# Attention of 16 heads over 512 keys with its scores computed once, stage semaphores cleared one block later, a router's counting in bf16, and another order in the last block

## The reference, cut to what matters

```python
q, k, v = h @ wq, h @ wk, h @ wv             # (2, 512, 16, 64) each
scores = einsum('bqhd,bkhd->bhqk', q, k) / sqrt(64)
w = softmax(scores, axis=-1)
z = z + einsum('bhqk,bkhd->bqhd', w, v).reshape(2, 512, 1024) @ wo + bo
```

## Time and profile before

| what | us |
|---|---|
| three executions, median | 4797.91 |
| the profiled execution, its own time | 4793.56 |
| span of the profiled execution, first to last instruction | 4791.7 |
| granted TensorE clock over the span, share of full speed | 0.902 |
| from the start of the attention's first stage to the end of its main one | 341.9 |
| one of its 16 pairs of heads, in the middle | 19.12 |
| the router's counting on PE | 15.8 |

### The profile page before, as it was taken

How to read it: one execution, slowest core, us unless ns; L and a number is a source line. 1 busy time by engine, 2 the same in 40 slices (tenths; PEclk the granted TensorE clock), 3 DMA queues, 4 the chain that set the end, 5 groups by cost and what they waited for, 6 DMA issues and landing times. The chain is left out here.

```text
span 4791.7 us, 86667 instructions
## 1 busy us (share of the span) xinstructions
PE 4050.0 (85%) x24901; PEld 2629.4 (55%) x25261; DVE 3436.7 (72%) x17352; ACT 2225.4 (46%) x7299; POOL 396.3 (8%) x322
## 2 busy tenths in 40 slices
PE   8999999999999998938888888888874349789797
PEld 6888888888888887622333333333332235423356
DVE  6888888888888888547677777777764449744443
ACT  4555555555555555415555555555553212133232
POOL 0000000000000000020111111111100000023310
PEclk9999999999999999958888888888886559899998
DMA  0000000000000000122222222212210001100001
GB/s 29 2 2 2 2 2 2 2 2 2 2 2 2 2 2 2 34 60 52 48 52 48 52 48 52 45 44 47 44 33 5 4 1 38 35 10 11 8 14 40
DMA packets 80809, 105.31 MB, mean 22 GB/s; under 512 B 25599, under 2 KB 73914, under 8 KB 78395
## 3 DMA queue, kind: packets, MB, share of 16 engines
q1 hardware_dynamic: 80379, 100.28, 8.6%
HBM read 69.17 MB, written 30.26 MB: 21 GB/s over the span
## 5 line engine op out<-in xcount | busy, mean ns | idle before, releaser
L287 DVE CUSTOM_DVE_ANT_0 I-219junk<-I-215encw,I-218expo,I-227rec 128x77 f32<-128x77 f32 x3072 | 941.2, 356 | 6.3
L1315 DVE TENSOR_REDUCE I-41383nmax<-ps 128x1 f32<-128x512 f32 x768 | 500.9, 684 | 215.9 <-PE ps L984 209.4
L1203 ACT ACTIVATE I-41386prob<-ps 128x512 f32<-128x512 f32 x768 | 428.4, 596 | 227.8 <-PE ps L1021 145.7
L265 ACT ACTIVATE I-217tanh_s<-ps 128x77 f32<-128x77 f32 x1024 | 241.3, 236 | 595.1 <-PE ps L245 595.1
L245 PE MATMUL ps<-I-212hist,I-49small 128*128 128x77 f32 x2048 | 456.5, 305 | 40.7 <-DVE I-212hist L323 40.6
L245 PEld LDWEIGHTS ps<-I-212hist,I-49small 128*128 128x128 f32 x2048 | 305.0, 188 | 296.4 <-DVE I-212hist L323 296.3
L251 PE MATMUL ps<-I-217tanh_s,I-49small 128*128 128x77 f32 x2048 | 454.8, 304 | 0.0
L252 PE MATMUL ps<-I-212hist,I-49small 128*128 128x128 f32 x2048 | 440.0, 297 | 0.0
L247 PE MATMUL ps<-I-212hist,I-216uh_h 128*128 128x128 f32 x2048 | 439.8, 296 | 0.0
L984 PE MATMUL ps<-I-41377kS,I-41376qS 96*128 96x512 bf16 x768 | 331.2, 457 | 127.8 <-DVE I-41383nmax L1315 58.7
L273 ACT ACTIVATE I-223hh<-I-229gate_t,I-228pre,I-222rh 128x1 f32<-128x1 f32 x1024 | 395.3, 386 | 84.6
(11 more groups left out here) (534 smaller groups left out, 7254.4 us busy)
## 6 DMA issues: line engine op xcount, KB each, us to landing
I-41376qS<-parts SPq DMA_DIRECT2D x24, 768.0 KB, 7.5
parts<-I-41395room SPq DMA_DIRECT2D x36, 384.0 KB, 2.5
parts<-I-41395room SPq DMA_DIRECT2D x36, 256.0 KB, 2.2
I-41377kS<-parts SPq DMA_DIRECT2D x12, 768.0 KB, 7.9
parts<-I-41395room SPq DMA_DIRECT2D x36, 128.0 KB, 1.8
I-49small<-in_layers SPq DMA_DIRECT2D x6, 768.0 KB, 9.0
I-66646w<-in_blocks SPq DMA_DIRECT2D x8, 514.0 KB, 7.1
I-41376qS<-I-41385mrow SPq DMA_DIRECT2D x192, 2.0 KB
```

The source lines that it names most:

```text
L287: return e.tensor_tensor_reduce(junk[:, 2 * g + b, :], encw[:, g, b, :], expo[:, b, :], inv[:, b:b + 1], rec[:, b, g:g + 1], ALU.mult, ALU ...
L1203: e.activation(prob[:, tau % 2, j, :], k.ps[:, b, :], ACT.Exp, scale=scale).then_inc(free[b], 1)
L1315: e.tensor_reduce(nmax[:, U % HG, i, j:j + 1], k.ps[:, use[0], :], AX.X, ALU.max, negate=True).then_inc(free[use[0]], 1)
```

## The change

`stage` no longer clears its semaphores before a second barrier. The clears stand behind the block and are followed by no barrier, so POOL executes them at the head of the next stage while the other engines go on; the semaphores themselves are given back only when the next block has ended. At the end of the program one barrier stays.

`attention3` is replaced by `self_attention`, whose unit is one tile of 128 queries of a pair of heads: 64 units, unrolled. Per unit: two score matmuls (queries on partitions); DVE takes the maximum of both heads and scales it; ACT takes the exponential with the maximum as bias and sums over the keys at the same time (`accum_out`); DVE inverts the two sums per query; POOL multiplies the probabilities by them; PE transposes 8 tiles; ACT copies those of head 0 and DVE those of head 1 to SBUF; two matmuls per key tile multiply by V with all 512 queries. The first stage of before is gone, `wos` is loaded behind the third weights.

```diff
@@ stage
-        for sem in sems:
-            nc.gpsimd.sem_clear(sem)
-        nc.all_engine_barrier()
+    with nc.Block() as block:
+        yield block, sems
+    release()
+    for sem in sems:
+        nc.gpsimd.sem_clear(sem)
+    HELD.append(ctx)
@@ router
-        mask = sbuf(ctx, nc, "mask", [P, NT, E])
+        mask = sbuf(ctx, nc, "mask", [P, NT, E], BF16)
-                    for i in range(NT):
-                        for j in range(i + 1):
-                            mm = e.matmul(psp[:, i // TPB, i % TPB, :], k.tri if j == i else k.ones, mask[:, j, :],
-                                          start=(i % TPB == 0 and j == 0), stop=(j == i), skip_group_check=True)
+                    e.matmul(earlier, tri_b[:], mask[:], start=True, stop=False, skip_group_check=True)
+                    for j in range(NT - 1):
+                        mm = e.matmul(earlier[:, j + 1:, :], ones_b[:], mask[:, j:j + 1, :].to_broadcast([P, NT - 1 - j, E]),
+                                      start=False, stop=(j == NT - 2), skip_group_check=True)
...
-                    link(e.max(best[:, i, :], pr[:, i, :]))
+                    e.max(best[:, i, :], pr[:, i, :]).then_inc(s.best, 1)
...
-                    for b in range(B):
-                        link(e.tensor_scalar(keepb[:, b], psp[:, b], float(capacity), None, ALU.is_lt))
+                    link(e.tensor_scalar(keep[:], earlier, float(capacity), None, ALU.is_lt))
@@ self_attention (new), tensor
+                def flip(u):
+                    e.wait_ge(s.divided, u + 1)
+                    for a in range(2):
+                        if u:
+                            e.wait_ge((s.flat0, s.flat1)[a], u)
+                        for c in range(TPB):
+                            mm = e.transpose(k.ps[:, 6 + a, c * P:(c + 1) * P], prob[:, u % 3, a, c * P:(c + 1) * P], k.ident)
+                        mm.then_inc(s.flipped, 1)
...
+                for t in range(NU + PV):
+                    G, i = divmod(t, TPB)
+                    if t < NU:
+                        score(t)
+                    if i < 3 and G + 1 < NG:
+                        project(G + 1, i)
+                    if 0 <= t - LAG < NU:
+                        flip(t - LAG)
+                    if t >= PV:
+                        weigh(*divmod(t - PV, TPB))
@@ scalar
+                def raise_(u):
+                    e.wait_ge(s.topped, 2 * u + 2)
+                    if u >= 3:
+                        e.wait_ge(s.flipped, 2 * (u - 2))
+                    for a in range(2):
+                        e.activation(prob[:, u % 3, a, :], score_ps(u)[:, a, :], ACT.Exp, scale=scale,
+                                     bias=nmax[:, u % 2, a:a + 1], accum_out=total[:, u % 3, a:a + 1]).then_inc(s.raised, 1)
...
+                for t in range(NU + LAG):
+                    G, i = divmod(t, TPB)
+                    if i < 3 and G + 1 < NG:
+                        keep(G + 1, i)
+                    if t < NU:
+                        raise_(t)
+                    if t >= LAG:
+                        flatten(t - LAG)
@@ vector
+                def top(u):
+                    e.wait_ge(s.scored, u + 1)
+                    if u >= 2:
+                        e.wait_ge(s.raised, 2 * (u - 1))
+                    e.tensor_reduce(nmax[:, u % 2, :], score_ps(u), AX.X, ALU.max, negate=True).then_inc(s.topped, 1)
+                    e.wait_ge(s.topped, 2 * u + 1)
+                    e.tensor_scalar(nmax[:, u % 2, :], nmax[:, u % 2, :], scale, None, ALU.mult).then_inc(s.topped, 1)
...
+                for t in range(NU + PV + 1):
+                    G, i = divmod(t - PV, TPB)
+                    if t < NU:
+                        top(t)
+                    if G >= 1 and i == 0:
+                        keep_out(G - 1)
+                    if 0 <= t - LAG < NU:
+                        flatten(t - LAG)
+                    if t < NU:
+                        invert(t)
@@ gpsimd
+                for u in range(NU):
+                    e.wait_ge(s.inverted, u + 1)
+                    e.tensor_tensor(prob[:, u % 3], prob[:, u % 3], inv[:, u % 3, :].unsqueeze(2).to_broadcast([P, 2, T]),
+                                    ALU.mult).then_inc(s.divided, 1)
```

More of the change, by code:

```diff
@@ L2678, in _ @@
                 e.activation(eq[:], low[:], ACT.Exp).then_inc(s.exps, 1)
-                e.wait_ge(s.rows, 1)
-                for b in range(B):
-                    e.activation(place_row[:, b * T:(b + 1) * T], k.ps[:, 2 + b, :], ACT.Copy).then_inc(s.place_row, 1)
                 def pick(n):
@@ L2692, in _ @@
                         pick(n + 1)
+                    if n == 0:
+                        e.wait_ge(s.rows, 1)
+                        for b in range(B):
+                            e.activation(place_row[:, b * T:(b + 1) * T], k.ps[:, 6 + b, :], ACT.Copy).then_inc(s.place_row, 1)
                     if n < E:
@@ L2718, in link @@
                     e.wait_ge(s.step, done[0])
-                e.wait_ge(s.logits, 1)
-                link(e.tensor_tensor(lg[:], scores, each(bias), ALU.add))
-                link(e.tensor_reduce(most[:], lg[:], AX.X, ALU.max))
-                e.tensor_tensor(low[:], lg[:], over(most), ALU.subtract).then_inc(s.lowered, 1)
                 e.wait_ge(s.consts, 1)
@@ L2729, in _ @@
                 done[0] += 4
[L2730 to L2733 removed]
+                e.wait_ge(s.step, done[0])
                 for j in range(NSLOT):
```

413 lines of the change are left out of this document (142 added, 271 removed).

## The result

| | before | after |
|---|---|---|
| median of the runs, us | 4797.91 | 4665.59 |
| all runs, us | 4793.68 to 4799.32 | 4665.13 to 4668.61 |
| span of the profiled execution, us | 4791.69 | 4666.76 |

Forecast: 4669, range 4650 to 4702. To see whether the sum is right for its reasons, I cut both traces at the stage ends, and compared stage by stage the time from first to last work, and the idle time of all engines between two stages.

The account below looks back on a forecast made before the run. No engine was taken to bound the whole kernel; PE bounded the old attention. Gains of 75 (attention), 40 (stage ends), 15 (routers), less 1 (last block), made 129 us: 4664.6 on the profiled scale, 4669 on the median's, range 4650 to 4702.

Parts of the forecast that it names:

- The loop that was forecast: Attention: DVE's small scaling multiplication waits for POOL's multiplication; then exponentials, reciprocal and hand-overs, 1.8 us, make a 3.8 us period.
- P: Attention: time of POOL's multiplication of the probabilities per unit, taken as 2.0 us.
- flatten (and every fourth unit keep_out) fit beside the exponentials: Attention, DVE: these steps were taken to fit beside ACT's two exponentials, 1.5 us, adding nothing to the loop.
- PE's own price: Attention: PE's scores, transpositions, products with V and projections, 14.8 us a pair, 3.71 us a unit.
- PE bounds the attention: Rival: two elements don't take the ports, or POOL's multiplication is under 1.9 us; 4660 us in all; chance 0.18.
- 3.8 a unit: Attention: period of one of 64 units, set by the loop through POOL; 4.15 us upper end, PE's 3.71 lower.
- The start and the end: Attention: time of the stage outside its 64 unit periods, taken as 23 us (18 to 31).
- One meeting of the engines, 0.25: Stage ends: one of two engine meetings goes at each of 63 ends, 0.25 us each, 15.8 us.
- For the clears the forecast had 31 us: Stage ends: 434 semaphore clears at 0.072 us each leave the path, 31.2 us.
- The 3.4 us behind the transformer: Stage ends: the addition behind the transformer ends late, waiting for POOL's 67 clears; 3.4 us lost.
- in full: Last block: the row of slots and two gathers, 8.8 us, follow in full behind gather 0's wait; expert 0 1.1 us later.

Follow-up runs that it names:

- the runs with the long multiplication: Changed kernel with POOL's multiplication over 2 x 768 columns instead of 2 x 512: 4725.10 us; the same without DVE's multiplication by 0.125: 4659.68 us.
- the run without the small multiplication: Changed kernel without DVE's multiplication of two numbers by 0.125, the scale put into ACT's copy of q: 4660.67 us, ratio 0.9711 to the kernel before.
- the run with the barrier: Changed kernel with one barrier of all engines added behind each block, clears left in place: 4690.10 us, ratio 0.9779 to the kernel before.

## Why the prediction was right, point by point

**The total**: 4669 forecast, 4665.6 measured. By the two traces the gain is 125 us where the sum had 129. Most terms came for their reasons, but they missed both ways, and that the misses partly cancelled is luck.

**Attention, 75 forecast, 70 found** (70 to 74 by the lengths that the same stage took in other runs). In the pairs the clock stayed at 1.00. The loop that was forecast is there, POOL's multiplication and then 1.8 us, and the runs with the long multiplication show it as directly as can be: 59 us of the stage with the same POOL work, by taking away one multiplication of two numbers. But it doesn't set the period alone. In the changed kernel it shows in two units of four, PE is idle 0.25 us of a pair, and either bound by itself gives nearly the same time. The Trainium skill ("SBUF — State Buffer", Who interferes with whom) says that the pair of ports is held for a whole instruction; the small multiplication that ends within 0.03 us of POOL agrees; two elements a partition are enough for it. Two sizes of the loop were off. P was 1.89 and not 2.0, 7 us too much over 64 units. And the step "flatten (and every fourth unit keep_out) fit beside the exponentials" is wrong for `keep_out`: it holds up PE. Where the loop alone bounds (both heads' products left out) it stands behind the blocked instruction, and the fourth unit takes 4.35 us in place of 3.68, 11 us over 16 pairs. These partly cancel, which left 3.85 a unit for the loop.

PE's own price was off as well: 14.8 us a pair forecast, 15.12 with nothing in its way. The term that was too small is the scores. They took 0.96 us from start to start before a matmul of the same shape in rows 2; here they stand before matmuls of all 128 rows and take 1.06 (4239.44 to 4240.50), 0.4 us more a pair. The trace of before had that price too, in the same pair (timeline, PE), where the scores stand before a product with V:

```profile
4342.60 1.13 PE L2129 MATMUL ps<-I-62535kk,I-62533q 64*128 64x512 f32 x4
4343.66 1.08 PE L2176 MATMUL ps<-I-62543prob,I-62536V 128*64 128x512 f32 x4
```

At a granted clock of 1.00 this order took 1.06 us in all 15 cases of that stage, and scores before scores 0.96 in all 44. The Trainium skill ("TensorEngine Tiling (Array Packing)", Key Properties) says that changing the tiling mode drains the engine. These times fit; that draining is the cause isn't shown. So the rival "PE bounds the attention" was as near to the truth as the forecast: the two bounds, 15.38 and 15.12 to 15.24, stand 1 or 2% apart, and the pair of 15.44 meets both. That the forecast's 3.8 a unit came out is luck in so far as PE's own 3.78 would have given it too. The start and the end took 271.7 - 16 x 15.44 = 25 us against 23; the run without the small multiplication shows that some 6 of them were the loop again, in the units that have few or no products with V, and some 3 the clock at the start.

**Stage ends, 40 forecast, 40.7 found.** The sum holds and its split doesn't. "One meeting of the engines, 0.25" is 0.35 by the run with the barrier, 21 us of 41. For the clears the forecast had 31 us, less 2.3 for the last stage's and some 4 lost again, so 25; the runs leave 20. The 3.4 us behind the transformer came as forecast, and go when the clears are put off.

**Routers, 15 forecast, 15.6 found**, the counting 2.1 us against 2.3. **Last block, 1 us lost forecast, 0.4 found**: gather 0 waits 2.5 us for its pieces of `to_slot` (forecast 2.4) and the slots come 1.2 us sooner (1.3), but row and gathers take 0.9 us less than "in full", because the clock is higher by then. The forecast had no term for that.

**Not forecast**: 9 us in the products behind short ends, through the clock, less 1.7 in other stages. The view for it was at hand, rows of the same stage before, with the clock at 0.85 or 0.61. I priced idle time as idle time only.

**Open**: the transformer's stage. Its code is the same in all kernels. It took 1533.5, 1532.0 and 1539.0 us in the three profiles with the old ends, and 1538.8 to 1545.4 in the eleven with the new ones. The medians are 9 us apart and the ranges touch. The difference grows at several places of the stage and not at its start. It goes in part with the clock that was granted: 0.857 and 0.855 over the two shortest stages, 0.843 and 0.846 over the two longest. With one profile of each kernel I can't say whether the new ends cause it. If they do, the ends are worth 40.7 + 7.2 - 8.7 = 39 us with the clock's part, and 48 otherwise; the measured 43 and 42 us lie between.

## What to carry to other kernels

Price a unit of a software pipeline by each engine's busy time and by the loop through its hand-overs, and put every instruction into the loop that stands behind a blocked one in its engine's order, not only those that feed it. When an engine looks 98% busy, that alone doesn't make it the bound: take work off it and see whether the period follows; here 2 us less of matmuls gave 0.06 us, and the other bound taken away 0.2, because the two lay side by side. And look for the price of an instruction in the order in which it will stand: the scores were 0.1 us dearer before another shape, and the trace of before had both. And before giving a tiny SBUF to SBUF instruction of DVE a place beside long POOL work, look for an earlier instruction that can carry its factor for nothing.

## What the runs showed of the hardware

- A multiplication of 128x2 f32 on DVE takes 0.17 us alone, and 1.67 to 1.77 us in 37 of 64 units beside a POOL instruction of 2.75 us; where it is held, it ends 0.02 to 0.03 us behind POOL. The maximum over 128x1024 from PSUM takes 1.22 us beside either.
- POOL's multiplication takes 1.89 us for 1024 elements a partition and 2.75 for 1536, so 1.67 ns for each one more.
- Two matmuls that use 64 columns of the array each run side by side: leaving out one of two took nothing off PE. The Trainium skill ("TensorEngine Tiling (Array Packing)", Key Properties) says that tiles work in parallel, and the trace agrees.
- Behind an attention, a product that started after 1.05 or 1.42 us of idle PE ran at 1.00 throughout; after 2.44 us the clock fell for part of it, and after 4.46 us it ran at 0.86 in the mean. A small product ran at 1.00 where the clock rose in the stage ahead, and at 0.55 where it rose 4.07 us into the product.
- Two heads' scores over 512 columns (64 rows each) take 0.96 us before another such pair and 1.06 us before matmuls of 128 rows.
- A barrier of all engines costs 0.35 us here.
